# Expert blocks in four interleaved runs, with weights fetched by indirect loads

## What is computed

```python
logits = x2d @ gate_w.T                       # 32 experts
rw = softmax(logits); _, sel = top_k(sigmoid(logits), 4)
w = take_along_axis(rw, sel); w = w / w.sum()
g = einsum('th,ehi->eti', x, Wg); u = einsum('th,ehi->eti', x, Wu)
a = silu(g) * u * cw.T[:, :, None]            # cw: the tokens' weights, 0 where not chosen
out = einsum('eti,eih->th', a, Wd)            # and the same with 16 small experts, times 0.05
```

## Time and profile before

| | us |
|---|---|
| median of 3 runs | 1832.52 (1831.14 to 1833.46) |
| the profiled execution's own time | 1829.17 |
| its span (first to last instruction) | 1827.3 |
| block loop of the experts, from the first weight load to the last y stored | about 265 to 475 |

### The profile page before, as it was taken

How to read it: one execution, slowest core, us unless ns; L and a number is a source line. 1 busy time by engine, 2 the same in 40 slices (tenths; PEclk the granted TensorE clock), 3 DMA queues, 4 the chain that set the end, 5 groups by cost and what they waited for, 6 DMA issues and landing times. The chain is left out here.

```text
span 1827.3 us, 26569 instructions
## 1 busy us (share of the span) xinstructions
PE 1490.5 (82%) x9515; PEld 1342.5 (73%) x9518; DVE 1190.9 (65%) x2464; ACT 993.3 (54%) x2084; POOL 513.9 (28%) x442
## 2 busy tenths in 40 slices
PE   5788638888236899989999989999988999999846
PEld 4777537777225888878888878888887888888723
DVE  3444458888335667776766666767666677677577
ACT  3333208787214556656565655655656656656545
POOL 2111113333424213232232232322322323222114
PEclk9888859999657999999999999999999999999967
DMA  3011019999321101010110101110101001000020
GB/s 98 21 36 36 23 57 299 322 323 306 113 93 41 31 27 38 7 47 21 48 39 8 37 18 38 36 46 24 38 7 50 18 27 36 22 7 23 22 81 23
DMA packets 82969, 118.19 MB, mean 65 GB/s; under 512 B 15640, under 2 KB 67264, under 8 KB 82848
## 3 DMA queue, kind: packets, MB, share of 16 engines
q1 hardware_dynamic: 78288, 104.14, 17.6%
q0 software_dynamic: 4560, 12.46, 2.7%
HBM read 106.14 MB, written 10.42 MB: 64 GB/s over the span
## 5 line engine op out<-in xcount | busy, mean ns | idle before, releaser
L1427 ACT ACTIVATE ga_pT<-ga_ps_t 128x512 fp32r<-128x512 f32 (+1 forms) x512 | 244.0, 517 | 224.9 <-PE ga_ps_t L1657 224.9
L1695 PE MATMUL ga_ps_m<-ga_pT,ga_v 128*128 128x512 f32 (+1 forms) x832 | 312.1, 413 | 14.3 <-DVE ga_out_n L1579 12.6
L1601 PE MATMUL ga_ps_s<-ga_kT,ga_qT 128*128 128x400 f32 (+1 forms) x1536 | 309.1, 350 | 2.2 <-ACT ga_probs L1435 1.8
L1547 DVE TENSOR_TENSOR ga_pT<-ga_ps_t,ga_pT 128x512 fp32r<-128x512 f32 (+1 forms) x512 | 278.1, 581 | 40.5 <-ACT ga_pT L1427 39.2
L1435 ACT ACTIVATE ga_probs<-ga_ps_s,ga_neg_max 128x1200 f32<-128x1200 f32 (+1 forms) x256 | 235.4, 927 | 95.2 <-DVE ga_neg_max L1566 95.2
L1601 PEld LDWEIGHTS ga_ps_s<-ga_kT,ga_qT 128*128 128x128 f32 x1536 | 273.9, 189 | 3.8 <-ACT ga_probs L1435 2.2
L1657 PE MATMUL ga_ps_t<-all_eye,ga_probs 128*128 128x128 f32 (+1 forms) x1664 | 228.6, 274 | 9.2 <-DVE ga_kT L1543 7.6
L1697 PE MATMUL ga_ps_m<-ga_pT,ga_v 128*128 128x256 f32 (+1 forms) x832 | 235.2, 283 | 0.0
L1657 PEld LDWEIGHTS ga_ps_t<-all_eye,ga_probs 128*128 128x128 f32 (+1 forms) x1664 | 193.6, 141 | 23.1 <-DVE ga_kT L1543 11.2
L1695 PEld LDWEIGHTS ga_ps_m<-ga_pT,ga_v 128*128 128x128 f32 (+1 forms) x832 | 158.4, 190 | 50.4 <-issue 11.2
L1601 PE MATMUL ga_ps_t<-ga_w_in,ga_encT 128*128 128x256 f32 (+1 forms) x1248 | 172.1, 288 | 22.4 <-DVE ga_kn L1540 19.9
(11 more groups left out here) (274 smaller groups left out, 2573.2 us busy)
## 6 DMA issues: line engine op xcount, KB each, us to landing
ex_raw<-in_L_ffn_packed SPq DMA_DIRECT2D x63, 704.0 KB, 6.2
ga_w_raw<-in_L_xattn_Wq SPq DMA_DIRECT2D x16, 512.0 KB, 4.1
ga_w_raw<-in_L_xattn_Wo SPq DMA_DIRECT2D x16, 512.0 KB, 4.7
ga_inv_rows<-ga_inv_row SPq DMA_DIRECT2D x64, 128.0 KB, 3.2
ex_y_rows<-ex_y SPq DMA_DIRECT2D x63, 128.0 KB, 4.9
ca_cache<-in_ctx SPq DMA_DIRECT2D x4, 1536.0 KB
ga_enc<-in_ctx SPq DMA_DIRECT2D x12, 512.0 KB, 5.7
ga_w_kv_raw<-in_L_xattn_Wk SPq DMA_DIRECT2D x16, 128.0 KB, 3.2
```

What stands on the lines that cost most here:

```text
L1427: nc.scalar.activation(dst(HI), src, ACT.Copy, scale=scale).then_inc(read, 1)
L1547: nc.vector.tensor_tensor(dst(LO), src, f32(dst(HI)), ALU.subtract).then_inc(empty, 1)
L1601: mm = nc.tensor.matmul(out, lhs(a), rhs(c), start=first and n == 0, stop=last and n == 2)
L1695: nc.tensor.matmul(ps_m[:, :, :], values[0:top, HI, tile, :], pT[0:top, :, tile, :], start=tile == 0, stop=False)
```

## The change

Two things are changed together.

1. The order of the blocks. Step j no longer computes block j but block `order[j]` = (j % 4) * 16 + j // 4: four runs of 16 consecutive blocks (0 to 15, 16 to 31, 32 to 47, 48 to 62), taken in turn. As step j uses buffer `raw[j % 4]`, each buffer sees one run.
2. The weight loads move from SP's queue to POOL's and become indirect loads of 128 rows of 5632 B, row numbers in `weight_row_u`, with a bounds check. DVE works the rows out: expert * 128 + lane at a run's first block and wherever the expert changes from the block before; otherwise, and for unused blocks, a number past the end, which the load skips without moving anything. The load still signals its semaphore.

POOL's order becomes: loads 0 to 3, gathers 0 to 2, then in turn gather i + 3 and load i + 4. SP only stores y, in order. ACT's, DVE's and PE's block loops are as they were: every block still converts its buffer with lines 714 and 852.

The diff, without the declarations of the new small tiles:

```diff
--- before.py
+++ after.py
@@ -492,6 +492,9 @@
     HALVES = T // BANK
     RAWS, WS, XGS, YS, BACK = 4, 5, 4, 3, 3
     AHEAD = 3
+    RUN = SLOTS // RAWS
+    order = [(j % RAWS) * RUN + j // RAWS for j in range(NBLK)]
+    assert sorted(order) == list(range(NBLK))
     assert D == 2 * P and NBLK == 63 and packed.shape[2] == COLS and HALF == 112 and T == 2 * BANK
 
     with ExitStack() as ctx:
@@ -611,7 +618,7 @@
         turned_moves.append((ps_a[:, 0, 0:DC * E].rearrange("p (c e) -> p c e", c=DC),
                              lambda s: gateT[:, s, :, :]))
         ps_rank = ps_y[:, 1, 0:(TT + 1) * E].rearrange("p (t e) -> p t e", e=E)
-        ps_row = ps_a[0:1, 1, 0:SLOTS]
+        ps_row = ps_a[:, 1, 0:SLOTS]
         ps_token = ps_x[:, 0, 0:2 * SLOTS].rearrange("p (m b) -> p m b", m=2)
 
         block = ctx.enter_context(nc.Block())
@@ -621,21 +628,10 @@
             sp.dma_start(gate[:, :], gate_w).then_inc(gate_in, 16)
             sp.wait_ge(xn_ready, TT)
             sp.dma_start(xn_rows.rearrange("(t p) d -> p t d", p=P), xn[:, :, :]).then_inc(xn_stored, 16)
-            sp.wait_ge(dve_routed, EXPERT_ROW)
-            for j in range(NBLK + 2):
-                if j < NBLK:
-                    e = sp.value_load(expert_row[0:1, j:j + 1], min_val=0, max_val=E - 1)
-                    if j >= RAWS:
-                        sp.wait_ge(w_lo, j - RAWS + 1)
-                    sp.dma_start(raw[j % RAWS][:, :], packed[bass.ds(e, 1), :, :].rearrange("e p i -> p (e i)")
-                                 ).then_inc(raw_in[j % RAWS], 16)
-                s = j - 2 - RAWS
-                if s >= 0:
-                    sp.wait_ge(y_here, s + 1)
-                    sp.dma_start(y_rows[s * P:(s + 1) * P, :], y[s % YS][:, :]).then_inc(y_stored[s % YS], 16)
-            for s in range(NBLK - RAWS, NBLK):
+            for s in range(NBLK):
+                at = order[s] * P
                 sp.wait_ge(y_here, s + 1)
-                sp.dma_start(y_rows[s * P:(s + 1) * P, :], y[s % YS][:, :]).then_inc(y_stored[s % YS], 16)
+                sp.dma_start(y_rows[at:at + P, :], y[s % YS][:, :]).then_inc(y_stored[s % YS], 16)
 
         @block.gpsimd
         def _(pool):
@@ -672,9 +668,20 @@
                 if j >= XGS:
                     pool.wait_ge(x_turned, j - XGS + 1)
                 nc.gpsimd.indirect_dma_start(xg[j % XGS][:, :], None, xn_rows[:, :],
-                                             bass.IndirectOffsetOnAxis(ap=token_u[:, j:j + 1], axis=0)
+                                             bass.IndirectOffsetOnAxis(ap=token_u[:, order[j]:order[j] + 1], axis=0)
                                              ).then_inc(xg_in[j % XGS], 16)
 
+            def load(j):
+                if j >= RAWS:
+                    pool.wait_ge(w_lo, j - RAWS + 1)
+                at = order[j]
+                nc.gpsimd.indirect_dma_start(raw[j % RAWS][:, :], None, packed.rearrange("e p i -> (e p) i"),
+                                             bass.IndirectOffsetOnAxis(ap=weight_row_u[:, at:at + 1], axis=0),
+                                             bounds_check=E * P - 1, oob_is_err=False).then_inc(raw_in[j % RAWS], 16)
+
+            pool.wait_ge(dve_routed, EXPERT_ROW)
+            for j in range(RAWS):
+                load(j)
             pool.wait_ge(xn_stored, 16)
             pool.wait_ge(dve_routed, TOKENS)
             for j in range(AHEAD):
@@ -682,6 +689,8 @@
             for i in range(NBLK):
                 if i + AHEAD < NBLK:
                     gather(i + AHEAD)
+                if i + RAWS < NBLK:
+                    load(i + RAWS)
 
             for i in range(YS):
                 pool.wait_ge(y_stored[i], 16 * len(range(i, NBLK, YS)))
@@ -819,19 +828,31 @@
             nc.vector.tensor_tensor(in_block[:, :, :], block_row_b[:, :].unsqueeze(1).broadcast_to([P, PAIRS, SLOTS]),
                                     slot_block_b[:, :].unsqueeze(2).broadcast_to([P, PAIRS, SLOTS]), ALU.is_equal
                                     ).then_inc(dve_routed, 1)
-            then(nc.vector.tensor_scalar(passed[:, :], ends[0:SLOTS, :], lane[0:SLOTS, 0:1], None, ALU.is_le))
-            settled()
-            then(nc.vector.tensor_reduce(block_expert[:, :], passed[:, :], AX.X, ALU.add))
-            settled()
-            nc.vector.tensor_scalar(block_expert[:, :], block_expert[:, :], float(E - 1), None, ALU.min
-                                    ).then_inc(dve_routed, 1)
+            then(nc.vector.tensor_scalar(passed[:, 0, :], ends[0:SLOTS, :], lane[0:SLOTS, 0:1], None, ALU.is_le))
+            then(nc.vector.tensor_scalar(passed[:, 1, :], ends[0:SLOTS, :], lane[0:SLOTS, 0:1], None, ALU.is_lt))
+            then(nc.vector.tensor_reduce(run_first[:, :], eye[0:SLOTS, 0:SLOTS].rearrange("p (r b) -> p r b", b=RUN)[:, :, 0],
+                                         AX.X, ALU.add))
+            settled()
+            then(nc.vector.tensor_reduce(block_expert[:, :], passed[:, :, :], AX.X, ALU.add))
+            settled()
+            then(nc.vector.tensor_tensor(again[:, :], block_expert[:, 0:1], block_expert[:, 1:2], ALU.is_equal))
+            settled()
+            then(nc.vector.tensor_scalar(block_expert[:, 1:2], block_expert[:, 0:1], float(E - 1), None, ALU.min))
+            then(nc.vector.tensor_scalar(again[:, :], again[:, :], float(E), block_expert[:, 0:1], ALU.mult, ALU.add))
+            settled()
+            then(nc.vector.tensor_tensor(row_base[:, :], block_expert[:, 1:2], again[:, :], ALU.subtract))
+            settled()
+            nc.vector.scalar_tensor_tensor(row_base[:, :], row_base[:, :], run_first[:, 0:1], again[:, :], ALU.mult, ALU.add
+                                           ).then_inc(dve_routed, 1)
             for n in range(TOP):
                 at = slice(n * TT, (n + 1) * TT)
                 nc.vector.tensor_tensor(in_lane[:, at, :], lane_row_b[:, :].unsqueeze(1).broadcast_to([P, TT, P]),
                                         slot_lane_b[:, at].unsqueeze(2).broadcast_to([P, TT, P]), ALU.is_equal
                                         ).then_inc(in_lane_ready, 1)
             dve.wait_ge(pe_routed, EXPERTS_TURNED)
-            nc.vector.tensor_copy(expert_row[:, :], ps_row).then_inc(dve_routed, 1)
+            then(nc.vector.tensor_scalar(weight_row[:, :], ps_row, float(P), lane[:, 0:1], ALU.mult, ALU.add))
+            settled()
+            nc.vector.tensor_copy(weight_row_u[:, :], weight_row[:, :]).then_inc(dve_routed, 1)
             then(nc.vector.tensor_copy(slot_u[:, :], slot[:, :]))
             dve.wait_ge(exp_ready, 1)
             then(nc.vector.tensor_reduce(top_sum[:, :], top_exp[:, :, :], AX.X, ALU.add))
@@ -920,7 +941,8 @@
                                       hits_b[:, t:t + 1, :].broadcast_to([P, TT - t, E]), start=False, stop=t == TT - 1)
             mm.then_inc(pe_routed, 1)
             pe.wait_ge(dve_routed, EXPERTS)
-            nc.tensor.transpose(ps_row, block_expert[:, :], eye[0:SLOTS, 0:SLOTS]).then_inc(pe_routed, 1)
+            nc.tensor.transpose(ps_row, row_base[:, :].broadcast_to([SLOTS, P]), eye[0:SLOTS, 0:SLOTS]
+                                ).then_inc(pe_routed, 1)
 
 
             pe.wait_ge(token_in_ready, 2)
```

More of the change, by code:

```diff
@@ L546, in experts @@
         in_lane = sb("in_lane", [P, PAIRS, P], BF16)
-        passed = sb("passed", [SLOTS, E])
-        block_expert = sb("block_expert", [SLOTS, 1])
-        expert_row = sb("expert_row", [1, SLOTS], U32)
+        passed = sb("passed", [SLOTS, 2, E])
+        block_expert = sb("block_expert", [SLOTS, 2])
+        run_first = sb("run_first", [SLOTS, 1])
+        again = sb("again", [SLOTS, 1])
+        row_base = sb("row_base", [SLOTS, 1])
+        weight_row = sb("weight_row", [P, SLOTS])
+        weight_row_u = sb("weight_row_u", [P, SLOTS], U32)
         lane_part = sb("lane_part", [P, SLOTS])
```

## The result

The changed kernel takes 1847.9 us, the median of 4 runs (1847.2 to 1851.0), beside 1831.8 us of the kernel before (4 runs on the same chip, 1830.9 to 1833.5). The ratio is 1.009, with an interval of 1.0073 to 1.0108: slower by 16 us, where 16 us of gain were forecast. 1847.9 lies outside the range of 1809 to 1832.

A forecast was written before the change was run, and what follows sets the result against it. The prediction took the DMA engines to bound the expert-block loop, with DVE, ACT and PE close behind. Its terms -20.1 + 0.5 + 3.5 = -16.1 us took the median of 1832.5 to 1816.4 us, range 1809 to 1832.

The forecast's parts named there:

- The bound of the kernel before: Expert-block loop: only the DMA engines are full, 0.983 MB a block at 319 GB/s, 3.08 us.
- The next bound, 2.75 us a block: Expert-block loop: once loads no longer bound it, the engines' cycle of releases holds it at 2.75 us a block.
- the ring: Expert-block loop: releases among DVE, PE and ACT taking 5.50 us for two blocks.
- Part 1: Weight loads: only 33 of 63 move, 21.6 MB go, and the loop gains 20.1 us.
- Part 2: Loads on POOL's queue: 0.95 to 1.1 us an issue, POOL's step 2.50 us, hidden under 2.75; +0.5 us.
- the hold by line 852: POOL's issues in the loop: transfers can't be written out while DVE runs line 852; 1896 us, chance 0.03.
- POOL's cover of 0.25 us: Expert-block loop: POOL's step of 2.50 us lies this far under the 2.75 us a block.
- The rate of POOL's queue: Loads and gathers on q0: 229 to 292 GB/s, costing 0 to +7 us, taken as +0.5.
- Part 3: Start of the loop: extra DVE work and four loads ahead of the first gather, +3.5 us, bounds +2 and +6.
- POOL becomes the bound outright: Expert-block loop: kernel slower, 1857 us by two descriptors a row or 1896 by a lock; chance 0.13.
- The skipped loads move something: Skipped weight loads: no traffic is saved, 1848 us, or +3.5 us at the rate of now; chance 0.05.
- The ring didn't loosen: Rival for the loop: without its 0.28 wait DVE needs 2.61 us a step, 1808 us; chance 0.06.

The follow-up runs named there:

- e4: Kernel before with the interleaved block order, SP issuing only the 33 loads that move, from a list fixed for this input: 1820.6 us, ratio 0.9938.
- e12: Changed kernel in the old block order, all 63 loads moving on POOL, weights_low reading one SBUF input (subtraction left out): 1821.3 us, ratio 0.9953.
- e10: Changed kernel with a POOL memset in place of each skipped load and weights_low reading one SBUF input (subtraction left out): 1816.1 us, ratio 0.9916.
- e1: Changed kernel with weights_low as a reduction reading one SBUF input instead of two (subtraction left out): 1859.0 us, ratio 1.0167.
- e13: Kernel before with its two-input weights_low cut into two operations of 704 columns: ratio 1.0010.
- e3: Kernel before with only the interleaved block order, all 63 loads still on SP: 1833.4 us, ratio 1.0009.
- e15: Changed kernel with weights_low reading one SBUF input (subtraction left out) and cut in two halves: 1814.4 us, ratio 0.9911.
- e6: Changed kernel with the 30 skipped loads not issued and weights_low reading one SBUF input (subtraction left out): 1828.3 us, ratio 0.9971.
- e7: Changed kernel in the old block order with all 63 loads moving on POOL's queue: 1854.1 us, ratio 1.0105.
- e11: Changed kernel with only the two-input weights_low cut into two operations of 704 columns: 1822.4 us, ratio 0.9967.
- e5: Changed kernel with the 30 loads that move nothing left out of the program by a fixed list: 1823.4 us, ratio 0.9954.
- e9: Changed kernel with a POOL memset in place of each of the 30 skipped loads: 1828.1 us, ratio 0.9982.
- e8: Changed kernel's order and skipping, but loads stay on SP, which branches at run time to load or only signal: 1823.4 us, ratio 0.9936.

## Why the prediction was wrong, point by point

**The bound of the kernel before** was named as the DMA engines. Taking bytes away did help (e4, -11 us), but less than -20.1. And e12, whose blocks need the same bytes, took 2.88 us a block. Its window beside that of the kernel before, 290 to 450 us (last two numbers: DMA share and GB/s):

```profile
290.00:450.00 160.00, 148.11 (x891) 129.81 (x891) 147.07 (x280) 137.80 (x279) 108.46 (x113) 1.00 0.99 339
```

339 GB/s at a share of 0.99, where I had read 319 GB/s at about 0.97 as full. A share near 1 wasn't a ceiling of 319 GB/s; the step "only the DMA engines are full" was right in direction and 6% too low in its rate.

**The next bound, 2.75 us a block**, was right. e10 comes to the ring undisturbed: line 883, its `weights_low`, starts at these times, the first and the third 5.49 us apart; from block 3 to block 62 a block takes 2.75.

```profile
402.08 1.62 DVE L883 TENSOR_REDUCE ex_w<-ex_raw 128x1408 fp32r<-128x1408 f32 x1 [0.24 <-ACT ex_w L733]
404.83 1.62 DVE L883 TENSOR_REDUCE ex_w<-ex_raw 128x1408 fp32r<-128x1408 f32 x1
407.57 1.62 DVE L883 TENSOR_REDUCE ex_w<-ex_raw 128x1408 fp32r<-128x1408 f32 x1
```

**Part 1** was right in its bytes, 21.6 MB of 21.6. In time it was too high: e4, which does this part alone, runs at 2.86 us a block and not 2.75. ACT's 9 waits for loads that are left, 6.1 us over the 56 blocks of the window, are 0.11 each and account for the difference.

**Part 2 is the step that failed.** The price of an issue was right as far as it went: 1.00 us for a load with nothing in its way (0.95 to 1.1 forecast), also for one that is skipped. The term of the sum that was mis-sized is the hold by line 852, set to nothing and kept as a rival with 0.03. It is 1.465 - 1.004 = 0.46 us on a load and 1.352 - 0.945 = 0.41 on a gather, means of the changed kernel against e1's, so a pair is 2.50 + 0.05 + 0.87 = 3.42 us. POOL's cover of 0.25 us is gone, and 0.67 over the ring is paid by nearly all of the 59 blocks. The measured pace is (487.15 - 290.23) / 59 = 3.34. Loop: 196.92 - 182.29 = +14.6 us, against -19.6 forecast for parts 1 and 2.

The rule was in hand and dismissed by a single row: the gather at 409.64 took its usual 0.94 beside line 852 at 410.17. But that gather starts 0.53 us *before* line 852. It shows what happens to an issue that comes first, and nothing of one that comes second. The upper bound of the issue, 2.28 us, was read as a gather behind unfinished ones; it starts at 271.05, within the `weights_low` from 270.88 to 272.50. The right test was every gather that starts within line 852: 13 rows, each ending 0.82 to 0.94 us after it. That the trace doesn't show the lock for the gathers, as the prediction has it, was a misreading. The rival's price, up to 4.1 us a step, was too high in turn: only the part of line 852 that lies ahead of an issue is paid, and not every issue meets it.

**The rate of POOL's queue** (+0.5) was no obstacle. In e12 its packets took 85.7% of 160 us and moved 46.93 MB, 342 GB/s by the same working that gave my bounds of 229 and 292.

**Part 3** had +3.5 us with bounds of 2 and 6; block 3's `weights_low` starts 6.3 us later. In the changed kernel's timeline:

```profile
258.22 0.23 DVE L831 TENSOR_SCALAR ex_passed<-ex_ends,ex_lane 64x32 f32<-64x32 f32 x1
258.36 3.65 DVE L832 TENSOR_SCALAR ex_passed<-ex_ends,ex_lane 64x32 f32<-64x32 f32 x1
258.38 3.60 POOL L662 TENSOR_TENSOR ex_token_in<-ex_in_block,ex_block_row_b 128x2048 bf16<-128x2048 bf16 x1 [34.17 <-DVE ex_in_block L828]
...
268.01 0.20 DVE L855 CAST ex_weight_row_u<-ex_weight_row 128x64 uint32<-128x64 f32 x1
...
269.19 1.26 POOL L678 DMA_INDIRECT ex_raw<-in_L_ffn_packed,ex_weight_row_u  x1 [7.21 <-DVE ex_weight_row_u L855]
...
274.65 0.97 POOL L670 DMA_INDIRECT ex_xg<-ex_xn_rows,ex_token_u  x1 [0.30 <-issue]
```

The first gather waits for four loads, (274.65 - 269.19) = 5.5 us, and PE's first transposes start at 281.64 and not at 277.6 to 279.0 (274.71 before). About 2 us of the delay are there before the changed lines begin: line 831, the first of them, starts at 258.22, and line 822, the same operation of the kernel before, at 256.14. These 2 us aren't the change's: e13 and e3, whose routing is that of before, start this operation at 258.14 and 259.85. Counted from it, block 3 comes 32.0 us later in place of 27.8: +4.2 us is the price of the start. Line 832 is the added comparison, 64 x 32 elements, and takes 3.65 us in place of some 0.2, as it stands beside a POOL operation until 261.98. In the kernel before the first `in_lane` operations met that stretch: all four took 7.71 us, and take 4.61 now, so most of it isn't new.

**Sum.** Loop +14.6 and start +6.3 make the last `weights_low` 20.9 us late; the span is 19.5 longer and the median 16.1. Forecast was -19.6 + 3.5 = -16.1. Of the 37 us between forecast and traces, 34 are the loop: 59 x (3.34 - 2.79) = 32 by the hold, if e15's pace is taken for the loop without it. 3 us are the start, 2 of them there before the changed lines. The medians differ by 32 us from the forecast; the rest is variation between executions.

**The rivals.** "POOL becomes the bound outright" is the case that came, by the lock and not by a second descriptor, and at 1848 us and not at 1857 or 1896. "The skipped loads move something" fell: 21.6 MB are gone, and their packets don't show in e15. The ring didn't loosen. Of the signs listed at the prediction's end, the bytes came as said (q0 +24 MB, q1 -45 MB), and the first sign of being wrong is what the profile shows: "A POOL without idle time in the loop, or loads over 1.2 us".

**Left open.** e1 and e6 have pauses of ACT of up to 2.5 us that no engine ends, 13 and 10 in the window of 160 us, and TensorE's granted clock is 0.91 on average in e1's window, where e15 has 1.00; whether it is a cause or comes of the pauses isn't known. e10, e12 and e15, with the same form of operation, have none, and e15 differs from e1 only by the cut in halves. The form isn't needed for them: e7, with two inputs, has one of 1.80 us at 300.93. What ACT waits for there isn't known. Nor is it settled how the gain of e11 divides between shorter holds and another meeting of issues and operations, or why the same bytes go faster with e12's queue than with SP's.

## What to carry to other kernels

Before work goes to GpSimd's queue, list what VectorE does in the meantime: here, each indirect DMA whose issue started at least 0.05 us into an operation with two SBUF inputs was held until that operation was over. So price the issue with the hold. Cutting that one operation in halves took 0.53 of the 0.87 us of hold away for 0.06 us of VectorE's time a block, and leaving the loads on SP's queue, with a branch at run time, avoided it. And a row speaks against a mechanism only if the order in it is the one that the change will bring: look for rows where the second one starts inside the first.

## What the runs showed of the hardware

- Between `weights_low` and an issue the hold goes one way: the operation takes 1.61 to 1.70 us whether an issue is under way or not. An issue that began earlier, or up to 0.04 us after it (e5: a gather 0.03 us after its start took 0.95), isn't held; one that starts 0.05 us after takes 2.46 in the changed kernel, one 0.15 us after takes 2.30. Two issues that came first are exceptions, and no run explains them: in e7 one that starts 0.14 us ahead of the operation takes 2.63 us, and in e11 one that starts 0.11 us ahead of a second half takes 1.82. Against a GpSimd operation that isn't a DMA it went the other way: line 832 took 3.65 us beside line 662, though it started 0.02 us ahead of it.
- An operation of the same kind with one input in SBUF and one in PSUM (lines 859 and 871 of the kernel before) doesn't hold an issue: 32 gathers that start within one take 0.94 or 0.95 us.
- By the Trainium skill (SBUF — State Buffer, Who interferes with whom) a GpSimd instruction that only writes isn't held by two SBUF inputs. The trace agrees: the 13 memsets of e9 that start within a two-input operation take 1.18 or 1.19 us, and e10's, beside one-input ones, 1.18. The same section has it as an inference that the issue of a DMA isn't held by such an operation, since it needs the write side. The measurement decides: it is held.
- An indirect load whose row numbers are all out of bounds moves none of its 0.721 MB by the packets of the queue (21.6 MB fewer for 30 loads), leaves 144 packets under 512 B, and still takes GpSimd 1.00 us to issue (e1).
- A branch at run time on SP ahead of each load cost nothing that can be told: e8 0.9936, the fixed list of e4 0.9938.
